# The Mamba stage of a decoder: two places per chunk for h, sums six chunks behind, and B tiles shared among three engines by a table

## The reference, cut to what matters

```python
xn = x * rsqrt(mean(x * x, -1) + 1e-6) * g
x_s, z = split(xn @ W_in.T)                     # 512 channels each
xc = silu(causal_conv4(x_s) + conv_b)
params = xc @ W_x.T                             # B: 16 states, C: 16 states, log_dt: 1
dt = softplus(log_dt @ W_dt.T + b_dt)           # per step and channel
A = -exp(A_log)
# per state s of 16:  h_s(t) = exp(dt * A_s) * h_s(t-1) + dt * B_s * xc
y = sum over s of h_s * C_s
y = (y + xc * D) * silu(z)
out = x + y @ W_out.T                           # then layernorm(x + out)
```

## Time and profile before

| what | value |
|---|---|
| median of 3 runs | 4200.27 us |
| the profiled execution, its time | 4201.03 us |
| its span | 4199.2 us |
| scans, first to last start (the Mamba stage) | 1342.4 to 3240.3 us |
| scans in it | 1024, of 1.211 us in the mean |
| one period of 64 steps, mid stage | 118.4 us |

### The profile page before, as it was taken

How to read it: one execution, slowest core, us unless ns; L and a number is a source line. 1 busy time by engine, 2 the same in 40 slices (tenths; PEclk the granted TensorE clock), 3 DMA queues, 4 the chain that set the end, 5 groups by cost and what they waited for, 6 DMA issues and landing times. The chain is left out here.

```text
span 4199.2 us, 73811 instructions
## 1 busy us (share of the span) xinstructions
PE 3510.9 (84%) x22848; PEld 2545.8 (61%) x22848; DVE 3128.6 (75%) x5241; ACT 2909.9 (69%) x5201; POOL 2717.5 (65%) x2890
## 2 busy tenths in 40 slices
PE   8996999989844888888888888888888799994666
PEld 5664666775422667666666666666667577762333
DVE  5666888844684788778878787787777477776988
ACT  2224888833565888887878888787887377774766
POOL 1224666610483998898989889898988355552555
PEclk9998999979867999999999999999999899997999
DMA  2111111151121111111111111111111111112111
GB/s 60 55 53 45 42 42 43 39 111 36 28 71 50 45 48 53 45 52 49 52 50 47 52 43 54 51 50 50 47 47 43 41 41 40 40 34 70 50 46 35
DMA packets 199386, 204.57 MB, mean 49 GB/s; under 512 B 45768, under 2 KB 164104, under 8 KB 199064
## 3 DMA queue, kind: packets, MB, share of 16 engines
q1 hardware_dynamic: 199064, 200.65, 16.3%
HBM read 149.18 MB, written 51.41 MB: 48 GB/s over the span
## 5 line engine op out<-in xcount | busy, mean ns | idle before, releaser
L2227 DVE TENSOR_TENSOR_SCAN ma_h<-ma_a,ma_pbu 128x512 f32<-128x512 f32 x1024 | 1223.2, 1211 | 344.9 <-PE ma_pbu L1825 180.2
L2123 POOL TENSOR_TENSOR ma_ch<-ma_h,ma_crep 128x512 f32<-128x512 f32 x1024 | 1338.1, 1324 | 201.3 <-DVE ma_h L2227 185.0
L1825 PE MATMUL ma_pbu<-ma_ident,ma_bu 128*128 128x128 f32 x4096 | 659.4, 285 | 175.9 <-DVE ma_h L2227 129.6
L1825 PEld LDWEIGHTS ma_pbu<-ma_ident,ma_bu 128*128 128x128 f32 x4096 | 484.5, 145 | 420.6 <-DVE ma_h L2227 279.6
L1834 PE MATMUL ma_py<-ma_ident,ma_ch 128*128 128x128 f32 x4096 | 637.9, 280 | 42.2 <-POOL ma_ch L2123 30.3
L2021 ACT ACTIVATE ma_a<-ma_dt,ma_A 128x510 f32<-128x510 f32 x1024 | 652.9, 717 | 1.4 <-issue 1.4
L2012 ACT ACTIVATE ma_bu<-ma_uT,ma_b_t 128x512 f32<-128x512 f32 x864 | 556.7, 718 | 11.8 <-PE ma_pbu L1825 10.1
L1834 PEld LDWEIGHTS ma_py<-ma_ident,ma_ch 128*128 128x128 f32 x4096 | 492.0, 145 | 70.2 <-POOL ma_ch L2123 64.4
L856 POOL TENSOR_TENSOR xa_prob<-xa_e,xa_rec_head 128x616 f32<-128x616 f32 x256 | 307.3, 1217 | 310.7 <-DVE xa_rec_head L945 309.9
L936 DVE TENSOR_REDUCE xa_top<-xa_pS 128x8 f32<-128x616 f32 x256 | 202.9, 793 | 149.6 <-PE xa_pS L625 142.2
L765 ACT ACTIVATE xa_eT<-xa_pE 77x512 f32<-77x512 f32 x512 | 276.7, 594 | 49.3 <-PE xa_pE L637 47.5
(11 more groups left out here) (312 smaller groups left out, 7312.0 us busy)
## 6 DMA issues: line engine op xcount, KB each, us to landing
ma_crep<-ma_ct_dram SPq DMA_DIRECT2D x256, 256.0 KB, 3.2
xa_x<-act SPq DMA_DIRECT2D x64, 256.0 KB, 2.6
act<-xa_y SPq DMA_DIRECT2D x64, 256.0 KB, 2.2
la_x<-in_x SPq DMA_DIRECT2D x32, 256.0 KB, 2.6
act<-la_y SPq DMA_DIRECT2D x32, 256.0 KB, 2.2
ea_x<-act SPq DMA_DIRECT2D x32, 256.0 KB, 11.9
act<-ea_x SPq DMA_DIRECT2D x32, 256.0 KB, 4.0
ma_x<-act SPq DMA_DIRECT2D x16, 512.0 KB, 4.5
```

Source lines behind the costliest of these rows:

```text
L1825: last = pe.transpose(pbu[c % 2][:, t * P:(t + 1) * P], bu[:, s % 2, t, c * P:(c + 1) * P], ident[:, :])
L2123: pool.tensor_tensor(ch[:, s % 2, c], h[:, c], crep[:, s % 4, :], ALU.mult).then_inc(multiplied, 1)
L2227: dve.tensor_tensor_scan(out=h[:, c, :], data0=a[:, s % 2, c, :], data1=pbu[c % 2][:, :], initial=0.0, op0=ALU.mult, op1=ALU.add).then_inc ...
```

## The change

- `h` gets two places per chunk (by s): the scan of step i waits for the product of step i - 8. The head start of the semaphore `multiplied` and the waits on it move by 4 accordingly. `yv` no longer has a tile of its own: it shares `one_av`.
- The sums stand 6 steps behind (LAG). The last six of a group stand one each in steps (0,0) to (1,1) of the next; the group's own sums start at step 9, two to a step until they have caught up. `gate` moves to before (1,2) and (1,3), two tiles each.
- B tiles: a table says how many tiles of a state VectorE makes (new `scale_tile` there, a `tensor_scalar` right after a scan of the state before) and how many GpSimd makes. VectorE gets 12 per group, GpSimd 4 in place of 10, ScalarE 48 in place of 54.
- `turn_b` goes from (7,3) to (9,2) and through pm[0]; `copy_b` on ScalarE from state 8 to state 10. The wait of `project_out` on `b_copied` is gone.
- Other places: `turn_gated` (2,2) to (3,2); `project_out` (4,1) to (5,1) and (8,0) to (8,3); `project_z` one half per step at states 12 to 14; `turn_u`; `y_stats`, `y_var`, `rstd_of`; `step_input` packed into (11,0) to (13,0); `squares` at states 11 to 13; `rms_of` at (14,1), `rms_diagonal` at (15,1); `step_log` half 1 before half 0 in the text, at states 11 and 10.

```diff
-        h = sb("h", [P, IC, GS])
+        h = sb("h", [P, 2, IC, GS])
-        yv = sb("yv", [P, IC, GS])
+        yv = one_av
-        def on_pool(s):
-            return 1 <= s <= 10
+        DVE_TILES = {1: 1, 6: 1, 7: 2, 8: 2, 9: 2, 10: 2, 11: 1, 15: 1}
+        POOL_TILES = {2: 1, 3: 1, 4: 1, 5: 1}
...
-            def turn_b(n, first):
-                if type(n) is int and n == 0:
-                    pe.wait_ge(z_copied, TT)
-                elif not first:
-                    pe.wait_ge(y_ready, 2 * n - 3)
+            def turn_b(n):
+                pe.wait_ge(l_used, 2 * n + 2)
                 for t in range(TT):
-                    last = pe.transpose(pm[1][:, t * P:(t + 1) * P], ct[:, t * P:(t + 1) * P], ident[:, :])
+                    last = pe.transpose(pm[0][:, t * P:(t + 1) * P], ct[:, t * P:(t + 1) * P], ident[:, :])
...
-                    if on_pool(s):
-                        pe.wait_ge(tile_ready, 10 * g + s)
+                    if s in DVE_TILES:
+                        pe.wait_ge(dve_tile_ready, tiles_until(DVE_TILES, N) * g + tiles_until(DVE_TILES, s))
+                    if s in POOL_TILES:
+                        pe.wait_ge(pool_tile_ready, tiles_until(POOL_TILES, N) * g + tiles_until(POOL_TILES, s))
...
                 if t == 2 and piece == 0:
-                    if prep:
-                        pe.wait_ge(b_copied, g + 3)
-                    else:
-                        pe.wait_ge(y_ready, 2 * g + 1)
+                    pe.wait_ge(y_ready, 2 * g + 1)
...
+            GATED = {(2, 2): 0, (2, 3): 1, (3, 1): 2, (3, 2): 3}
+            OUT = {(4, 1): (0, 0), (4, 2): (0, 1), (5, 0): (1, 0), (5, 1): (1, 1),
+                   (8, 0): (2, 0), (8, 1): (2, 1), (8, 2): (3, 0), (8, 3): (3, 1)}
+            PARAMETERS = {(6, 2): 0, (6, 3): 1, (7, 0): 2, (7, 1): 3}
+            Z = {(12, 0): (0, 0), (12, 1): (0, 1), (12, 3): (1, 0), (13, 0): (1, 1),
+                 (13, 2): (2, 0), (13, 3): (2, 1), (14, 1): (3, 0), (14, 2): (3, 1)}
+            U = {(13, 1): 0, (14, 0): 1, (14, 3): 2, (15, 0): 3}
...
-                        late = IC * s + c - 5
-                        if late >= 0:
-                            sum_state(g, late // IC, late % IC)
-                        if s == 0 and not first:
-                            for k in ((-1, 0), (1, 2), (3,), ())[c]:
-                                sum_state(g - 1, N - 1 if k >= 0 else N - 2, k % IC)
+                        at = IC * s + c
+                        if at < LAG and not first:
+                            late = K - LAG + at
+                            sum_state(g - 1, late // IC, late % IC)
+                        for _ in range(2):
+                            if at >= LAG + 3 and done <= at - LAG:
+                                sum_state(g, done // IC, done % IC)
+                                done += 1
...
+            SQUARES = {11: (0,), 12: (1, 2), 13: (3,)}
...
+            INPUTS = {(11, 0): (0, 0), (11, 1): (0, 1), (11, 2): (1, 0), (11, 3): (1, 1),
+                      (12, 1): (2, 0), (12, 2): (2, 1), (12, 3): (3, 0), (13, 0): (3, 1)}
-                        if (s, c) in ((6, 2), (10, 0)) and not first:
+                        if (s, c) in ((6, 1), (9, 3)) and not first:
                             rstd_of(g - 1, 0 if s == 6 else 1)
-                        if s == 5 and c == 2 and ahead:
+                        if s == 14 and c == 1 and ahead:
                             rms_of(g + 2)
-                        if s == 7 and c == 2 and ahead:
+                        if s == 15 and c == 1 and ahead:
                             rms_diagonal(g + 2)
...
+            def scale_tile(g, par, s, k):
+                if s == 1:
+                    dve.wait_ge(uT_copied, IC * g + IC)
+                    dve.wait_ge(b_copied, g + 1)
+                dve.wait_ge(bu_turned, K * g + (IC * s + 4))
+                t = TT - 1 - k
+                dve.tensor_scalar(bu[:, s % 2, t, :], uT[:, par, t, :], b_t[:, par, t, s:s + 1], None,
+                                  ALU.mult).then_inc(dve_tile_ready, 1)
...
+            STATS = {(5, 2): 0, (5, 3): 1, (9, 0): 2, (9, 1): 3}
+            FINISH = {(7, 0): 0, (7, 1): 1, (10, 2): 2, (10, 3): 3}
-                        if not first and (s, c) in ((0, 3), (1, 0)):
-                            for t in (2 * s, 2 * s + 1):
+                        if not first and (s, c) in ((1, 2), (1, 3)):
+                            for t in (2 * c - 4, 2 * c - 3):
                                 gate(g - 1, 1 - par, t)
-                        if prep and (s, c) in ((9, 1), (10, 1)):
+                        if prep and (s, c) in ((9, 3), (10, 1)):
                             one_plus(n, s - 9)
                         scan(g, s, c)
+                        if c < DVE_TILES.get(s + 1, 0):
+                            scale_tile(g, par, s + 1, c)
```

More of the change, by code:

```diff
@@ L1715, in group @@
                         store_c(g + 1, 1 - par)
-                    if s == 8 and not first:
+                    if s == 9 and not first:
                         store_y(g - 1, 0)
@@ L1891, in group @@
                                 project_x(n, s - 1, k)
[L1892 to L1895, removed]
+                        if (s, c) in GATED and not first:
+                            turn_gated(g - 1, GATED[s, c], prep)
+                        if (s, c) in OUT and not first:
+                            project_out(g - 1, *OUT[s, c])
                         if s in (6, 10) and c < 2:
                             add_skip(par, c + (2 if s == 10 else 0))
-                        if prep and (s, c) in ((6, 2), (6, 3), (7, 0), (7, 1)):
-                            parameters(n, 1 - par, (c + 2) % 4)
-                        if prep and (s, c) == (7, 2):
+                        if (s, c) in PARAMETERS and prep:
+                            parameters(n, 1 - par, PARAMETERS[s, c])
+                        if (s, c) == (7, 2) and prep:
                             spread_l(n)
[L1902 to L1909, removed]
+                        if (s, c) == (9, 2) and prep:
+                            turn_b(n)
+                        if (s, c) in Z and prep:
+                            project_z(n, *Z[s, c], first)
+                        if (s, c) in U and prep:
+                            turn_u(n, U[s, c])
             pe.wait_ge(w_loaded, 16 * len(loads))
@@ L1922, in _ @@
             spread_l(0)
-            turn_b(0, True)
+            turn_b(0)
             for c in range(IC):
@@ L1926, in _ @@
             groups(pe, group)
-            for late in range(K - 5, K):
+            for late in range(K - LAG, K):
                 sum_state(NG - 1, late // IC, late % IC)
@@ L1944, in copy_z, with squares @@
                 act.activation(sz[:, par, t, :], pm[1][:, :], ACT.Copy).then_inc(z_copied, 1)
-            def squares(n):
+            def squares(n, tiles):
                 act.wait_ge(x_loaded, 16 * n + 16)
-                for t in range(TT):
+                for t in tiles:
                     act.activation(square[:, t, :], x[:, t, :], ACT.Square, accum_out=ssq[:, t:t + 1]).then_inc(ssq_ready, 1)
@@ L2035, in group @@
                             copy_xT(n, c)
[L2036 to L2039, removed]
+                    if s in SQUARES and ahead:
+                        squares(g + 2, SQUARES[s])
+                    if s in (3, 4) and not first:
+                        copy_gated(g - 1, 2 * s - 5)
                     if s == 7 and prep:
                         copy_parameters(n)
-                    if s == 8 and prep:
-                        copy_b(n, np_)
                     if s == 9 and prep:
```

83 lines of the change are left out of this document (47 added, 36 removed).

## The result

The changed kernel takes 4160.56 us (median of 4 runs, 4158.71 to 4165.93) against 4200.35: ratio 0.9908, 95% interval 0.9891 to 0.9926. That is 40 us less; 49 were forecast. The profiled execution took 4165.93 us.

What follows compares the result with a forecast made beforehand. No engine is full; four nearly equal loads hold each other up, differing by stretch. Terms -1.3 + 1.15 - 3.4 + 0.25 give -3.3 us a period, 15 times -49.5, so 4151 us; range 4078 to 4208.

Steps and rivals of the forecast that it cites:

- C: Steps (6,0) to (9,0), 25.7 us, VectorE busy only 15.6: -3.4 us a period, bounds -4.5 and -1.0.
- A: Steps (11,0) to (2,0) of the next group, 49.6 us, bound by GpSimd: -1.3 us a period, bounds -3.4 and +1.5.
- B: Steps (2,0) to (6,0), 28.5 us, TensorE's ring and VectorE's work about equal: +1.15 us a period, bounds 0.3 and 2.5.
- D: Steps (9,0) to (11,0), 14.7 us, VectorE busy 13.6: +0.25 us a period, bounds -0.6 and +2.
- `rstd` brings nothing: In C, the 2.13 us `rstd` wait at 2109.16 goes without gain, since ScalarE sets the scan at (8,0).
- only part of the tile comes back at (8,0): In C, `bu` of state 8 loses a 0.61 us tile, but `step_size` waits for `spread_l`: only 0.3 comes back.
- the two chains: In C: `parameters` through ScalarE to scan (8,0); `project_out`'s 2.45 us wait for `b_copied`, delaying later scans; (9,0) gains 3.4.
- my terms: In B: state 5's tile +0.25 us, one more statistic and the variance +0.65, `project_out` off (4,0) -0.2.
- the three tiles: In D, three VectorE tiles cost 1.65 us, at 0.55 each.
- Rival 1: Slower: VectorE tiles wait for GpSimd; gain used up at 1.02 us a tile; 4220 us at 1.2; chance 0.13.
- Rival 2: No difference: `rdiag` stall and GpSimd's backlog add, A 50.5 us, time 4185 to 4200 us; chance 0.10.
- Rival 3: Much faster: the engines' balance holds, A 46.2, C 21.2, B 28.8 us, time 4093 us; chance 0.22.

Runs made afterwards that it cites:

- b_back: The changed kernel with `turn_b` back at (7,3), `copy_b` at state 8 and `project_out`'s wait on `b_copied` put back: 4218.0 us, ratio 1.005.
- b_only: The kernel before with only `turn_b` and `copy_b` moved as in the change and `project_out`'s wait on `b_copied` removed: 4201.1 us, ratio 1.0004.
- b_plus: b_only with `one_plus` at (9,3) in place of (9,1): 4177.9 us, ratio 0.9947 to the kernel before.
- rms_idle: The changed kernel with `squares` at state 7 and both `rms_of` and `rms_diagonal` at (7,3): 4153.4 us, ratio 0.9893 to the kernel before.
- rms_tile2: rms_idle with the tile of state 2 made by ScalarE instead of GpSimd: 4134.0 us, ratio 0.9845 to the kernel before.
- h_single: The changed kernel with one place of `h` per chunk again, so a scan waits for the product four steps back: 4170.1 us, ratio 0.9931.

## Why the prediction was right, and where its steps were off

Direction and place held, and the size roughly: 4151 forecast, 4160.6 measured, with C the source. But the single steps are less good than the sum. Over the 15 periods of the two profiled executions, in us:

| stretch | forecast x 15 | measured |
|---|---|---|
| A | -19.5 | +5.2 |
| B | +17.3 | +14.2 |
| C | -51.0 | -45.4 |
| D | +3.8 | -12.9 |
| sum | -49.5 | -38.9 |

A missed by 25 us and D by 17 the other way. That the sum came within 11 us is in part luck.

- C: -3.4 forecast, -3.5 measured in the period shown. That `rstd` brings nothing, that only part of the tile comes back at (8,0) (0.4 us, 0.3 forecast), and that the two chains end together at (9,0), all stand in the trace. It is 45 and not 51 us in all because the first group, which has no `project_out`, gains nothing and C was not 25.7 in every other group before (24.1 in two). b_back confirms that the wait is what C was longer by. What I did not see is that alone it would be given back in D (b_only): my sum has no term for it, and the change escapes it because `one_plus` moves too (b_plus).
- B: +1.15 forecast, +0.9 measured: 0.43 in state 2, where I put 0.44 for `turn_gated`, and 0.50 in state 5, where my terms make 0.7.
- D: +0.25 forecast, -0.7 measured. Mis-sized: the three tiles cost 0.37, 0.39 and 0.55 us (start to start) and not 0.55 each, and `one_plus` at (10,1) takes 0.68 us, no longer 1.17, since GpSimd no longer stands in front of it.
- A: -1.3 forecast, +0.8 measured in the period shown, the step that failed. I said that packing `step_input` closes 1.2 us of gaps, taking them for waits on inputs. They are four waits of 0.3 us of GpSimd on its own `dt` instruction, and they are all still there (1.24 us in all, after 1.17). The rest is slowing: GpSimd's list from the product of (11,0) to the tile of state 2 takes 48.2 us and not 46.4. Both new stalls came where I put them, `rdiag` (1.65 us, 2 to 4 forecast) and the tile of state 2 (1.57), but not in each group; rms_idle took out the first and rms_tile2 the second. I had no term for the lower clock behind the first, about 1.5 us in four of the 15 periods.
- The count: I multiplied one period by 15. Inside the body A grew by 1.6 us in the mean and across the body's end it shrank by 1.0. h_single says whose the second is: with one place of h it is gone.
- Rival 1, tiles stuck behind GpSimd: 567 ns in the mean, below the 1020 from which it decides. Tiles do wait (1.60 us in A), but one right behind a scan mostly comes first. Rival 2 had A right: 50.5, and it is 50.4 to 52.0 in the body; its time did not come, since C and D gained. Rival 3 was not reached: A never fell under 46.8 with the norms and the tile gone.

## What to carry to other kernels

A stall on the critical path may be the cover of the next engine's load: take it out alone and look at the stretch behind it before you count the gain; here the same edit was worth 0 alone, 22 us with one more call moved, and 57 inside the whole change. In a stretch where one engine never pauses, count its list, with the pauses that it makes for itself, and put movable work where that engine waits. Measure every period, not one, and put the granted clock beside each: equal work took two different times here, and one period shows only one of them.

## What the runs showed of the hardware

- The end of a loop's body costs. In the kernel before, TensorE had 12 waits, 32.0 us, in the stage, two at each of the six ends, which the profile puts down to no other engine; writing the groups out took 26 us off the changed kernel. What comes late there (the branch itself or the instructions behind it) no run tells apart.
- Behind a wait TensorE may work at half its rate for a while, the lower of its two levels (1.2 and not 2.4 GHz), or it may not. After the same wait of 3.08 us in b_back, four products took 1.91 us in one group and 1.03 in another, and C took 1.67 us more with the first. After the same wait of 1.65 us for `rdiag`, eight transposes took 2.06 and 1.15. Across the body's end two waits follow each other, 3.08 us and 2.16, and four turns behind them take 1.06 us in place of 0.60:

```profile
2164.72 0.65 PE L1829 MATMUL ma_pbu<-ma_ident,ma_bu 128*128 128x128 f32 x4 [3.08 <-issue]
2167.52 1.01 PE L1838 MATMUL ma_py<-ma_ident,ma_ch 128*128 128x128 f32 x4 [2.16 <-POOL ma_ch L2141]
2168.33 1.06 PE L1829 MATMUL ma_pbu<-ma_ident,ma_bu 128*128 128x128 f32 x4
```

- The same VectorE `tensor_scalar` of 128x512 took 0.46 us ahead of a GpSimd product and up to 1.60 where GpSimd's instructions followed one another without a pause; one of 128x1024 took 0.68, and 1.49 behind `rms_diagonal`. When VectorE came first (the tile at 2115.59), GpSimd's product took 1.44 us and not 1.27:

```profile
2115.75 1.44 POOL L2141 TENSOR_TENSOR ma_ch<-ma_h,ma_crep 128x512 f32<-128x512 f32 x1 [0.80 <-DVE ma_h L2245]
```

- GpSimd pauses 0.24 to 0.33 us where it waits for the end of its own instruction: 56 of 56 times behind `dt`, in both kernels.
